# A Mamba and RWKV layer: scans that begin from zero, with the carry added into dbx by GpSimd

## The chip, the core and the metric

The kernel runs on one core of a Trainium2 chip. Such a core has five engines with instruction queues of their own: TensorE (PE, matrix products and transposes, which write to PSUM), VectorE (DVE), ScalarE (ACT), GpSimd (POOL) and SyncE (SP, which here issues the transfers). They run at the same time and wait for one another through semaphores. The metric is the device time of one launch in microseconds, from three runs; a separate run under the hardware profiler gives the trace that the rows below come from. Of that trace a row "in a view by line" gives a source line, an engine, what is written and read, how often, the busy time and the mean time of one; a row of a timeline gives the start, the duration and the same names.

## The reference, cut to what matters

The input is x of 4 x 2048 x 256 in fp32. The layer is a layer norm, a selective state-space block (Mamba) with a second layer norm behind it, a residual, a third layer norm and an RWKV channel mix. The part that costs most is the scan over the tokens, with 16 states for each of 256 channels:

```python
delta = softplus(delta_raw @ W_dt + b_dt)
A = -exp(A_log)
dA  = exp(einsum('bld,dn->bldn', delta, A))
dBx = einsum('bld,bln->bldn', delta * x, B_ssm)
def step(h, inp):
    dA_t, dBx_t, C_t = inp
    h = dA_t * h + dBx_t
    y_t = einsum('bdn,bn->bd', h, C_t)
    return (h, y_t)
```

Around it stand `y + x * D`, the gate `y * silu(z)`, the product with W_out, the norms, and the channel mix `sigmoid(xr @ W_r) * (relu(xk @ W_k)**2 @ W_v)`, where xr and xk mix each token with the one ahead of it.

## The kernel before

The 8192 tokens are cut into 16 chunks of 512, four to a sequence (`NT = 16`, `CPB = 4`). A step t of the main loop scans chunk t, prepares chunk t+1 (normalises it, turns it, makes delta, u = delta * x, B and C, z), finishes the Mamba block of chunk t-1 and the channel mix of chunk t-2. Steps 0 and 15, a short step ahead and a closing part are cut down versions of it.

Within a step there are 16 *columns*, one for each state n. A column is 128 partitions x 2 halves (of the 256 channels) x 512 tokens, and it takes:

- ScalarE: two exponentials, `da_ps<-delta,a_neg` (`exps`, line 662), each into one of three PSUM banks of a ring. The exponential of half-column k needs the bank that half-column k-3 used, so ScalarE may be at most three half-columns ahead. In a turn of 32 *places* (two for each column) ScalarE makes the exponential of column n+1 at place 2n + half, and then whatever else its table `ACT_TURN` puts at that place.
- GpSimd: `dbx<-u,b_ring` (`times_b`, line 543), one instruction of 128x1024, three columns ahead (`B_LEAD = 3`) into a ring of four (`X_RING = 4`).
- VectorE: two scans, `tensor_tensor_scan` (line 1045), one for each half, with state = da * state + dbx. Their start value is the constant 0.0 where a sequence begins (t divisible by 4) and otherwise `carry[:, n, h:h + 1]`, one number for each partition, that ScalarE copied out of the chunk ahead (`keep_carries`, line 668, and `keep_split_carry`, line 673).
- The product with C, `hg<-...,c_ring`: for *whole* columns GpSimd makes it (line 556, 128x1024, from SBUF into SBUF, one column behind); for *split* columns, listed in `SPLITS`, the scan stays in PSUM and VectorE makes the product, as one of 128x1024 (line 1052) where another piece of work stands between scan and product, as two of 128x512 (line 1061) otherwise. Even steps have 8 split columns, odd steps 9.
- TensorE: eight transposes of 128x128 that add the column to y (line 1331), up to two columns behind.

The other work of a step is placed by hand: `ACT_TURN` and `VEC_TURN` give a place from 0 to 31 to each stage of ScalarE and VectorE, `PE_TURN` a column to each of TensorE's, `BANK` one of three PSUM banks. Three stages of ScalarE change the function table, by `preload_act_table_set` in the code: `sp` at place 10 loads the softplus table, makes delta and loads the table with exp and tanh; `ln_exp` at place 20 loads the table with ln and exp. After that come the stages that take an inverse root by ln and exp (`rs1`, `rs2`, `rs3`; lines 620 and 622). The stage `tanh` (line 731) stands at place 19. Within one place the code runs through the stages in a fixed order, in which `rs1` stands ahead of `tanh`, and `tanh` ahead of `ln_exp`.

SyncE loads B and C in groups of four columns into rings of two groups (`load_b`, `load_c`), each after the last reader of the slot.

## Time and profile before

| | us |
|---|---|
| median of three runs | 941.3 (941.04 to 941.36) |
| the profiled execution | 941.56 |
| its span, first to last instruction | 939.8 |
| mean granted TensorE clock, share of full | 0.978 |

| engine | busy us | share |
|---|---|---|
| PE | 858.4 | 91% |
| DVE | 900.5 | 96% |
| ACT | 837.5 | 89% |
| POOL | 890.4 | 95% |

The span is nearly the whole of the time, so what is read from the trace carries over. A duration of two or more instructions in a timeline runs from the first start to the last end; the next instruction often starts some 0.07 us before the last one ends, so what an instruction costs its engine is the distance from start to start (called pitch below). `L1144`, VectorE's gate, runs once in a step at nearly the same place; it starts at 93.5 us in step 1 and at 866.8 us in step 15, so 14 turns take 773.3 us, 55.24 us each. This stretch is called the steady part.

### The profile page before, as it was taken

How to read it: one execution, taken by the hardware profiler on the slowest of the kernel's cores; microseconds unless marked ns; L12 is line 12 of the kernel's file. 1: busy time of each engine (PE TensorE's matmuls, PEld its weight loads, DVE VectorE, ACT ScalarE, POOL GpSimd, SP SyncE). 2: the span in 40 equal slices, each digit the busy share in tenths (PEclk: the TensorE clock that was granted, in tenths of full speed). 3: DMA queues.
4: the chain of work that ended last, by engine and by line, in shares of the span. 5: the costliest groups of instructions: out<-in, count | busy, mean ns of one | idle time of the engine just before them, and what ended most of it. 6: DMA issues, size and time to landing. Idle time of an engine off the chain costs nothing.

```text
span 939.8 us, 15796 instructions
## 1 busy us (share of the span) xinstructions
PE 858.4 (91%) x5024; PEld 685.0 (73%) x5024; DVE 900.5 (96%) x986; ACT 837.5 (89%) x2007; POOL 890.4 (95%) x413
## 2 busy tenths in 40 slices
PE   8766679989999898989999898998999899899998
PEld 5545466867878586776868678786878768678876
DVE  5899999999999999999999999999999999999896
ACT  4776889999999999998999999998999999978875
POOL 4999999999999999999999999999999999999980
PEclk9977899999999999999999999999999999999999
DMA  7345435462644644454374634446354454445231
GB/s 229 149 179 204 180 135 205 180 242 103 226 157 156 225 178 159 183 190 181 150 248 156 224 140 174 166 179 248 144 194 182 144 195 180 157 161 224 90 103 45
DMA packets 49939, 163.60 MB, mean 174 GB/s; under 512 B 5249, under 2 KB 33153, under 8 KB 33601
## 3 DMA queue, kind: packets, MB, share of 16 engines
q1 hardware_dynamic: 48528, 161.27, 46.0%
q0 software_dynamic: 512, 1.31, 0.5%
q8 instruction: 40, 0.66, 0.3%
q14 instruction: 43, 0.34, 0.1%
q10 hardware_dynamic: 816, 0.02, 0.1%
HBM read 153.15 MB, written 9.44 MB: 173 GB/s over the span
## 4 chain that ended last, share of the span: by engine, by line
PE 40%; ACT 27%; DVE 20%; issue 11%; POOL 1%; POOLq 0%; DVEq 0%; ACTq 0%
PE w_ps L1340 9%; ACT da_ps L662 9%; PE y_ps L1331 8%; DVE da_ps L1045 7%; PE w_ps L1364 5%; DVE hg L1045 4%; PE w_ps L1373 4%; PE w_ps L1376 4%; DVE hg L1052 4%; DVE hg L1061 3%; PE w_ps L1479 2%; ACT h_tok L599 2%; ACT zs L723 2%; PE w_ps L1382 2%; ACT xn_tok L599 2%
## 5 line engine op out<-in xcount | busy, mean ns | idle before, releaser
L543 POOL TENSOR_TENSOR dbx<-u,b_ring 128x1024 f32<-128x1024 f32 x255 | 599.7, 2379 | 2.0 <-DVE hg L1045 1.9
L662 ACT ACTIVATE da_ps<-delta,a_neg 128x512 f32<-128x512 f32 x512 | 340.2, 684 | 25.9 <-DVE hg L1052 8.6
L556 POOL TENSOR_TENSOR hg<-hg,c_ring 128x1024 f32<-128x1024 f32 x122 | 290.2, 2379 | 7.5 <-ACT carry L668 6.7
L1331 PE MATMUL y_ps<-ident,hg 128*128 128x128 f32 x2048 | 261.8, 278 | 10.4 <-POOL hg L556 10.2
L1331 PEld LDWEIGHTS y_ps<-ident,hg 128*128 128x128 f32 x2048 | 239.9, 144 | 37.4 <-issue 17.8
L1045 DVE TENSOR_TENSOR_SCAN da_ps<-da_ps,carry,dbx 128x512 f32<-128x512 f32 x203 | 249.5, 1270 | 3.5 <-ACT da_ps L662 3.5
L1045 DVE TENSOR_TENSOR_SCAN hg<-da_ps,carry,dbx 128x512 f32<-128x512 f32 x181 | 220.3, 1264 | 2.1 <-ACT carry L668 1.7
L1052 DVE TENSOR_TENSOR hg<-da_ps,c_ring 128x1024 f32<-128x1024 f32 x68 | 82.3, 1210 | 0.2
L1061 DVE TENSOR_TENSOR hg<-da_ps,c_ring 128x512 f32<-128x512 f32 x130 | 82.3, 673 | 0.0
L1045 DVE TENSOR_TENSOR_SCAN da_ps<-da_ps,dbx 128x512 f32<-128x512 f32 x64 | 75.4, 1211 | 3.4 <-ACT da_ps L662 3.1
L1045 DVE TENSOR_TENSOR_SCAN hg<-da_ps,dbx 128x512 f32<-128x512 f32 x64 | 74.8, 1206 | 2.4 <-ACT da_ps L662 2.4
L1340 PE MATMUL w_ps<-xnT_ring,w_in 128*128 128x512 f32 x120 | 61.7, 638 | 16.0 <-ACT xT L704 14.1
L1373 PE MATMUL w_ps<-w_rT,mixed 128*128 128x256 f32 x240 | 61.7, 380 | 0.0
L1376 PE MATMUL w_ps<-w_r_prev,mixed 128*128 128x256 f32 x240 | 61.6, 379 | 0.0
L1364 PE MATMUL w_ps<-w_in,xnT_ring 128*128 128x256 f32 x248 | 59.4, 382 | 0.9 <-ACT delta L696 0.6
L1340 PE MATMUL w_ps<-xnT_ring,w_dtx 128*128 128x512 f32 x120 | 57.9, 606 | 0.9 <-ACT bc_rows L808 0.9
L1364 PE MATMUL w_ps<-w_out,gated 128*128 128x256 f32 x248 | 58.7, 379 | 0.0
L1340 PE MATMUL w_ps<-mixed,w_kT 128*128 128x512 f32 x120 | 57.3, 601 | 0.0
L1364 PEld LDWEIGHTS w_ps<-w_in,xnT_ring 128*128 128x128 f32 x248 | 45.5, 190 | 15.0 <-ACT kact L690 4.9
L1373 PEld LDWEIGHTS w_ps<-w_rT,mixed 128*128 128x128 f32 x240 | 44.4, 190 | 11.4 <-issue 6.7
L1364 PE MATMUL w_ps<-w_vT,kact 128*128 128x256 f32 x232 | 52.6, 379 | 0.0
L1376 PEld LDWEIGHTS w_ps<-w_r_prev,mixed 128*128 128x128 f32 x240 | 45.6, 190 | 6.2
(214 smaller groups left out, 1320.7 us busy)
## 6 DMA issues: line engine op xcount, KB each, us to landing
c_ring<-bc_rows_dram SPq DMA_DIRECT2D x64, 1024.0 KB, 4.6
b_ring<-bc_rows_dram SPq DMA_DIRECT2D x63, 1024.0 KB, 6.6
xres<-in_L_attn_x_in_dram SPq DMA_DIRECT2D x16, 512.0 KB, 4.7
x_tok<-in_L_attn_x_in_dram SPq DMA_DIRECT2D x15, 512.0 KB, 6.0
out_dram<-r_out SPq DMA_DIRECT2D x14, 512.0 KB, 3.2
bc_rows_dram<-bc_rows SPq DMA_DIRECT2D x64, 16.0 KB, 5.4
w_in<-in_L_attn_W_in_dram SPq DMA_DIRECT2D x2, 256.0 KB, 4.3
x_tok<-in_L_attn_x_in_dram SPq DMA_DIRECT2D x2, 256.0 KB, 4.6
```

The source lines that it names most:

```text
L543: pool.tensor_tensor(dbx[:, n % X_RING, :, :], u[:, ip, :, :], b.to_broadcast([P, KH, LC]), ALU.mult).then_inc(s["dbx_done"], 1)
L556: pool.tensor_tensor(part, part, c_of(n).to_broadcast([P, KH, LC]), ALU.mult).then_inc(s["g_pool"], 1)
L599: last = act.activation(dst[j], src[j], ACT.Identity, scale=rs[j], bias=nm[j])
L662: act.activation(da_of(n, h), delta[:, ip, h, :], ACT.Exp, scale=a_neg[:, h, n:n + 1]).then_inc(s["da_ready"], 1)
L1045: dve.tensor_tensor_scan(out, da_of(n, h), dbx[:, n % X_RING, h, :], 0.0 if first else carry[:, n, h:h + 1], ALU.mult, ALU.add).then_inc(s ...
L1052: dve.tensor_tensor(hg[:, n % H_RING, :, :], da_both(n), c_of(n).to_broadcast([P, KH, LC]), ALU.mult).then_inc(s["g_vec"], 1)
L1061: last = dve.tensor_tensor(hg[:, n % H_RING, h:h + 1, :], da_ps[:, at:at + 1, :], c_of(n), ALU.mult)
L1331: last = pe.matmul(y_tok[:, b, h * P:(h + 1) * P], hg[:, n % H_RING, h, b * P:(b + 1) * P], ident[:, :], is_transpose=True, start=n == 0 a ...
L1340: last = pe.matmul(out, w[:, k, cols], x[:, k, :], start=k == 0, stop=k == KH - 1)
L1364: last = pe.matmul(by_block(out)[:, b, :], xT_[:, k, tokens], w[:, k, :], start=b == 0 and k == 0 and not begun, stop=k == KH - 1, skip_gr ...
L1373: pe.matmul(by_block(out)[:, b, :], h_of[:, k, at_b + 1:at_b + 1 + P], w_rT[:, k, :], start=k == 0, stop=False)
L1376: last = pe.matmul(by_block(out)[:, b, :], h_of[:, k, at_b:at_b + P], w_r_prev[:, k, :], start=False, stop=k == KH - 1)
```

## The change

Every scan now starts from 0.0. For chunks that continue a sequence, the start value is put in through the first token instead: da of the first token times the carry is added to dbx of the first token. For it

- ScalarE makes `first_a`, the exponential of delta's first token for all 16 states: two instructions of 128x16 right behind softplus in the stage `sp` (`first_decays`), in the 12 steps ahead of a chunk that continues a sequence;
- GpSimd multiplies carry and first_a for eight columns at a time (`weigh_carries`, 128x16, two for a chunk) and adds the product to the first tokens of two columns at a time (`hand_over`, 128x4, eight for a chunk), one of its places after it has made the two columns;
- GpSimd makes dbx for two columns in one instruction of 128x2048 (`times_b_twice`), except columns 0 and 1 of chunk 0. The ring grows to six columns, and the lead to four;
- VectorE's scan waits for `handed_over` where it waited for the carry;
- all even steps get column 3 as a ninth split column;
- places and banks are set anew, among them `rs1` from 22 to 19, `k0` from 9 to 8, `z1` from 11 to 13 on ScalarE, `gate` from 8 to 9, `u1` from 22 to 20 on VectorE, `xD`, `v0` and `v1` on TensorE; SyncE's loads stand in another order. Some semaphores of the closing part are shared between its two halves.

`C_RUN = 1` means that GpSimd's product with C is still one column an instruction. The core of the diff:

```diff
-X_RING = 4
+X_RING = 6
+HAND, WEIGH = 2, 8
+C_RUN = 1
-B_LEAD, C_LAG, Y_LAG = 3, 1, 2
+B_LEAD, C_LAG, Y_LAG = 4, 1, 2
-SPLITS = [[0, 2, 5, 6, 8, 11, 12, 14], [0, 2, 3, 5, 6, 8, 11, 12, 14]]
+SPLITS = [[0, 2, 3, 5, 6, 8, 11, 12, 14], [0, 2, 3, 5, 6, 8, 11, 12, 14]]
-                sum1=15, sq1=16, x0=18, tanh=19, ln_exp=20, rs1=22, x1=22, sq20=22, sq21=23, rs2=23, k1=24, square=24,
+                sum1=15, sq1=16, x0=18, tanh=19, ln_exp=20, rs1=19, x1=22, sq20=22, sq21=23, rs2=23, k1=24, square=24,
...
+            def weigh_carries(i, ip, n):
+                part = slice(n, n + WEIGH)
+                need(pool, s["first_a_set"], KH * firsts(i))
+                need(pool, s["carry_split"], kept_splits(i - 1, n + WEIGH - 1))
+                need(pool, s["carry_saved"], kept_wholes(i - 1, n + WEIGH - 1))
+                pool.tensor_tensor(handed[:, part, :], carry[:, part, :], first_a[:, ip, part, :],
+                                   ALU.mult).then_inc(s["handed_set"], 1)
+            def hand_over(i, ip, n):
+                pool.wait_ge(s["dbx_done"], NS * i + n + HAND)
+                pool.wait_ge(s["handed_set"], NS // WEIGH * (firsts(i) - 1) + n // WEIGH + 1)
+                at = dbx_of(i, n)
+                first = dbx[:, at:at + HAND, :, 0]
+                pool.tensor_tensor(first, first, handed[:, n:n + HAND, :], ALU.add).then_inc(s["handed_over"], 1)
+            def times_b_twice(i, ip, n):
...
+                need(pool, s["scan_done"], KH * (NS * i + n + 1 - X_RING + 1))
+                at, row = dbx_of(i, n), n % GN
+                b = b_ring[:, n // GN % BG, row:row + 2, :]
+                pool.tensor_tensor(dbx[:, at:at + 2, :, :], u[:, ip, :, :].unsqueeze(1).to_broadcast([P, 2, KH, LC]),
+                                   b.unsqueeze(2).to_broadcast([P, 2, KH, LC]), ALU.mult).then_inc(s["dbx_done"], 2)
...
+            def first_decays(i, ip):
+                need_all_read(act, i - 1, ["dt0", "dt1"])
+                for h in range(KH):
+                    act.activation(first_a[:, ip, :, h], a_neg[:, h, :], ACT.Exp,
+                                   scale=delta[:, ip, h, 0:1]).then_inc(s["first_a_set"], 1)
...
                         act.preload_act_table_set(EXP_TANH)
+                        if (t + 1) % CPB:
+                            first_decays(t + 1, nxt)
...
-                    dve.tensor_tensor_scan(out, da_of(n, h), dbx[:, n % X_RING, h, :],
-                                           0.0 if first else carry[:, n, h:h + 1], ALU.mult, ALU.add).then_inc(s["scan_done"], 1)
+                    dve.tensor_tensor_scan(out, da_of(n, h), dbx[:, dbx_of(t, n), h, :],
+                                           0.0, ALU.mult, ALU.add).then_inc(s["scan_done"], 1)
```

How the instructions stand in the two built programs, at three places. A row gives its number on the engine, the line, the operation, what is written and read, and its shape.

ScalarE, places 18 to 23 of a turn, ahead of the change (exponentials of columns 10 to 12; xT is the stage `x0` or `x1`, r_out is `tanh`, lv and rs are an inverse root, h_tok is `sq20`):

```order
302 L662 ACTIVATE da_ps<-delta,a_neg 128x512 x2
303 L704 ACTIVATE xT<-w_ps,d_par 128x512
304 L662 ACTIVATE da_ps<-delta,a_neg 128x512
305 L731 ACTIVATE r_out<-w_ps 128x512 x2
306 L662 ACTIVATE da_ps<-delta,a_neg 128x512
307 L873 ACT_TABLE_LOAD
308 L662 ACTIVATE da_ps<-delta,a_neg 128x512 x2
309 L668 ACTIVATE carry<-hg 128x4
310 L620 ACTIVATE lv<-sq,eps 128x4
311 L622 ACTIVATE rs<-lv 128x4
```

The same place behind the change:

```order
336 L726 ACTIVATE da_ps<-delta,a_neg 128x512 x2
337 L774 ACTIVATE xT<-w_ps,d_par 128x512
338 L726 ACTIVATE da_ps<-delta,a_neg 128x512
339 L684 ACT_TABLE_LOAD
340 L684 ACTIVATE lv<-sq,eps 128x4
341 L686 ACT_TABLE_LOAD
342 L686 ACTIVATE rs<-lv 128x4
343 L801 ACTIVATE r_out<-w_ps 128x512 x2
344 L726 ACTIVATE da_ps<-delta,a_neg 128x512
345 L945 ACT_TABLE_LOAD
```

The inverse root now stands ahead of tanh and of the load of line 945, and the built program has a table load ahead of its logarithm and another ahead of its exponential, which no line of the code asks for. Both stand there in steps 0 to 13, 14 times; the loads of the old places are all still there.

GpSimd in the middle of a chunk that continues a sequence, ahead of the change and behind it:

```order
50 L543 TENSOR_TENSOR dbx<-u,b_ring 128x1024 [waits u1_done,scan_done,u0_done,b_loaded3] x2
51 L556 TENSOR_TENSOR hg<-hg,c_ring 128x1024 [waits carry_saved,c_loaded2]
52 L543 TENSOR_TENSOR dbx<-u,b_ring 128x1024 [waits u1_done,scan_done,u0_done,b_loaded3]
53 L556 TENSOR_TENSOR hg<-hg,c_ring 128x1024 [waits carry_saved,c_loaded2]
54 L543 TENSOR_TENSOR dbx<-u,b_ring 128x1024 [waits u1_done,scan_done,u0_done,b_loaded3]
```

```order
49 L590 TENSOR_TENSOR dbx<-dbx,handed 128x4
50 L600 TENSOR_TENSOR dbx<-u,b_ring 128x2048
51 L615 TENSOR_TENSOR hg<-hg,c_ring 128x1024
52 L590 TENSOR_TENSOR dbx<-dbx,handed 128x4
53 L600 TENSOR_TENSOR dbx<-u,b_ring 128x2048
54 L615 TENSOR_TENSOR hg<-hg,c_ring 128x1024
55 L590 TENSOR_TENSOR dbx<-dbx,handed 128x4
```

Two columns of dbx became one instruction, and a small addition stands between them and the next two.

VectorE at columns 9 to 11, behind the change (the order of these is as before, but that the second `u` stood one column later, and the scans read carry):

```order
239 L1114 SCALAR_TENSOR_TENSOR hg<-da_ps,dbx 128x512 [waits y_added,da_ready,handed_over,dbx_done]
240 L1114 SCALAR_TENSOR_TENSOR hg<-da_ps,dbx 128x512 [waits da_ready]
241 L1114 SCALAR_TENSOR_TENSOR hg<-da_ps,dbx 128x512 [waits y_added,da_ready,handed_over,dbx_done]
242 L1114 SCALAR_TENSOR_TENSOR hg<-da_ps,dbx 128x512 [waits da_ready]
243 L1151 TENSOR_TENSOR u<-w_ps,delta 128x512 [waits work_ready0,work_read0]
244 L1114 SCALAR_TENSOR_TENSOR da_ps<-da_ps,dbx 128x512 [waits y_added,da_ready,handed_over,dbx_done]
245 L1114 SCALAR_TENSOR_TENSOR da_ps<-da_ps,dbx 128x512 [waits da_ready]
```

The scans are named SCALAR_TENSOR_TENSOR here. Whole columns 9 and 10, the stage `u1`, then split column 11 follow one another with no product of VectorE between them. Over the whole program the change makes 127 instructions of 128x2048 for dbx out of 254 of its 255 of 128x1024, leaves 114 products on GpSimd (122 before), adds 24 of 128x16 and 96 of 128x4 there, and leaves 16 products of 128x1024 and 250 of 128x512 on VectorE (68 and 130 before).

## Rows read from the trace of the kernel before

**Rows 1.** The page's engine totals; busy time by engine in the steady part
```profile
PE 858.4 (91%) x5024; PEld 685.0 (73%) x5024; DVE 900.5 (96%) x986; ACT 837.5 (89%) x2007; POOL 890.4 (95%) x413
...
core 0: us, PE busy (x) PEld busy (x) DVE busy (x) ACT busy (x) POOL busy (x), PEclk, DMA share, GB/s
93.50:866.80 773.30, 722.34 (x4290) 581.40 (x4289) 763.36 (x798) 721.97 (x1758) 764.60 (x343) 0.99 0.49 181
```

**Rows 2.** Timeline of ScalarE at places 19 to 22 of step 8
```profile
555.46 0.68 ACT L662 ACTIVATE da_ps<-delta,a_neg 128x512 f32<-128x512 f32 x1
556.07 1.07 ACT L731 ACTIVATE r_out<-w_ps 128x512 f32<-128x512 f32 x2
557.03 0.70 ACT L662 ACTIVATE da_ps<-delta,a_neg 128x512 f32<-128x512 f32 x1
557.74 1.28 ACT L873 ACT_TABLE_LOAD   x1
559.04 1.30 ACT L662 ACTIVATE da_ps<-delta,a_neg 128x512 f32<-128x512 f32 x2
...
560.37 0.28 ACT L620 ACTIVATE lv<-sq,eps 128x4 f32<-128x4 f32 x1
560.69 0.20 ACT L622 ACTIVATE rs<-lv 128x4 f32<-128x4 f32 x1
```

**Rows 3.** Timeline of VectorE in the same stretch, columns 8 to 11
```profile
552.21 1.21 DVE L1052 TENSOR_TENSOR hg<-da_ps,c_ring 128x1024 f32<-128x1024 f32 x1
553.33 0.68 DVE L1082 TENSOR_TENSOR u<-w_ps,delta 128x512 f32<-128x512 f32 x1
553.93 4.79 DVE L1045 TENSOR_TENSOR_SCAN hg<-da_ps,carry,dbx 128x512 f32<-128x512 f32 x4
558.65 2.44 DVE L1045 TENSOR_TENSOR_SCAN da_ps<-da_ps,carry,dbx 128x512 f32<-128x512 f32 x2
```

**Rows 4.** Groups of VectorE by line and form: scans into PSUM, from a carry and from zero
```profile
L1045 DVE TENSOR_TENSOR_SCAN da_ps<-da_ps,carry,dbx 128x512 f32<-128x512 f32 x203 | 249.5, 1270 | 3.5 <-ACT da_ps L662 3.5
...
L1045 DVE TENSOR_TENSOR_SCAN da_ps<-da_ps,dbx 128x512 f32<-128x512 f32 x64 | 75.4, 1211 | 3.4 <-ACT da_ps L662 3.1 <-POOL dbx L541 0.3
```

**Rows 5.** Timeline of VectorE where step 7 passes into step 8
```profile
514.03 2.32 DVE L1045 TENSOR_TENSOR_SCAN da_ps<-da_ps,dbx 128x512 f32<-128x512 f32 x2
516.26 1.26 DVE L1061 TENSOR_TENSOR hg<-da_ps,c_ring 128x512 f32<-128x512 f32 x2
517.44 1.21 DVE L1045 TENSOR_TENSOR_SCAN hg<-da_ps,dbx 128x512 f32<-128x512 f32 x1
...
521.26 2.46 DVE L1045 TENSOR_TENSOR_SCAN da_ps<-da_ps,carry,dbx 128x512 f32<-128x512 f32 x2
523.63 1.26 DVE L1061 TENSOR_TENSOR hg<-da_ps,c_ring 128x512 f32<-128x512 f32 x2
```

**Rows 6.** Groups of GpSimd by line and form
```profile
L543 POOL TENSOR_TENSOR dbx<-u,b_ring 128x1024 f32<-128x1024 f32 x255 | 599.7, 2379 | 2.0 <-DVE hg L1045 1.9
...
L561 POOL TENSOR_TENSOR nr<-nm,rs 128x4 f32<-128x4 f32 x14 | 3.0, 217 | 0.0
...
L541 POOL TENSOR_TENSOR dbx<-u,b_ring 128x512 f32<-128x512 f32 x1 | 1.3, 1262 | 0.9 <-DVE u L1082 0.9
...
L505 POOL TENSOR_SCALAR_AFFINE_SELECT ident<-ident 128x128 f32<-128x128 f32 x1 | 0.3, 283 | 0.2 <-POOL ident L503 0.2
```

**Rows 7.** Timeline of GpSimd around its one small instruction of a step
```profile
511.66 2.37 POOL L543 TENSOR_TENSOR dbx<-u,b_ring 128x1024 f32<-128x1024 f32 x1
513.97 0.22 POOL L561 TENSOR_TENSOR nr<-nm,rs 128x4 f32<-128x4 f32 x1
514.13 4.69 POOL L543 TENSOR_TENSOR dbx<-u,b_ring 128x1024 f32<-128x1024 f32 x2
```

**Rows 8.** Timelines of ScalarE and VectorE at the softplus stage of step 8
```profile
541.76 1.28 ACT L816 ACT_TABLE_LOAD   x1
...
543.26 0.69 ACT L662 ACTIVATE da_ps<-delta,a_neg 128x512 f32<-128x512 f32 x1
...
542.74 2.54 DVE L1045 TENSOR_TENSOR_SCAN da_ps<-da_ps,carry,dbx 128x512 f32<-128x512 f32 x2
```

**Rows 9.** Group of ScalarE by line: one of three table loads of a step
```profile
L813 ACT ACT_TABLE_LOAD x15 | 19.2, 1283 | 0.3
```

140 lines of the change are left out of this document (84 added, 56 removed).

## The prediction

> **What bounds the kernel now.** I read the engine totals first, then the same totals for the steady part alone (14 turns of 55.24 us) [rows 1]. There VectorE is busy 763.4 us and GpSimd 764.6 of 773.3, both near 99%; ScalarE is busy 722.0 and so idle for 51.3, or 3.7 us a turn. Two engines are full, and the third has little to spare. Next come the timelines of ScalarE and VectorE side by side [rows 2, 3], because the exponentials have only three PSUM banks: ScalarE can never be more than three half-columns, some 3.5 us of scans, ahead of VectorE. A pause of ScalarE longer than that is a pause of VectorE, whatever the share of busy time says. Let half-column (n, h) be half h of column n. The exponential at 555.46 is that of (10, 1), which needs the bank of (9, 0). That scan ran from 553.93 to about 555.1 (four scans in 4.72 us, 1.18 each) [rows 3], so ScalarE was then within 0.35 us of its farthest lead. It made tanh and (11, 0), done at 557.73 [rows 2]; VectorE read it at 558.65. The spare time there is 0.9 us.
>
> **VectorE: scans from zero.** Scans from a carry take 1270 ns and from zero 1211 in the groups by form [rows 4]. By start-to-start times a pair from zero costs 2.23 us (514.03 to 516.26) and a pair from a carry 2.37 (521.26 to 523.63) [rows 5]: 0.07 us a scan, 0.067 with other pairs of these turns. 384 scans lose it: -25.7. Column 3 of eight even steps comes over: two halves at 1.18 us (516.26 to 517.44) [rows 5], +9.4. And 52 products that were one instruction of 1.12 us (552.21 to 553.33) [rows 3] become two halves at 1.18, since their place holds no other work now: 52 x 0.05 = +2.6. VectorE's work changes by -13.7 us. The 32 scans of the last step don't count, because GpSimd, which gets more to do there, has no idle time in it to speak of: +2.1. This leaves -11.6.
>
> **GpSimd.** A column of dbx takes 2379 ns, the one half column of its kind 1262 [rows 6]: 1117 for 512 elements, and a fixed part of 2379 - 2 x 1117 = 145 ns. One of two columns saves that once: 127 x 0.145 = -18.4. Eight products at 2.31 us (511.66 to 513.97) [rows 7] go: -18.5. For the small ones the nearest row is the 128x4 instruction, which costs 0.16 us from start to start (513.97 to 514.13) [rows 7]: 96 x 0.16 = +15.4. The 24 of 128x16 are taken as 0.19: +4.6. Three hand-overs of a chunk stand (nearly) behind the very instruction whose result they wait for; an instruction that waited for its own engine's last result sat idle for 0.2 us [rows 6], and with the overlap of 0.07 us lost, that is 36 x 0.25 = +9. Sum: about -8 us, if none is dearer; the bounds are 0.16 and, with 0.2 of idle time on either side of each, 0.6 us. No wait of VectorE comes from it: two columns are made once the scan five columns ahead of the second is done, take 4.5 us, and with one product and the hand-over they are ready some 7 us later, while VectorE has four columns, over 13 us, to do. In the head and in step 0 it is the same instructions in another grain, at nothing.
>
> A rule on the price of the pair: the Trainium skill, GPSIMD Engine Reference, section "Performance versus the Vector engine", gives 4497 ns for a two-input operation of 2048 fp32. With the rows' durations the pair is 4613 ns; by the page's figure it would save another 0.12 us, 15 us of GpSimd's time in all. That would matter only if GpSimd were the bound, and it isn't in what follows.
>
> **ScalarE: two table loads that the places bring.** `rs1` moved from place 22 to 19, ahead of tanh and of the load at place 20. The table there is the one with exp and tanh, without ln, and the built program loads a table ahead of the logarithm and again ahead of the exponential. Every table load of the trace takes 1283 ns [rows 9], 1.30 from start to start (557.74 to 559.04) [rows 2]. Logarithm and exponential cost 0.32 (560.37 to 560.69) and about 0.15 [rows 2]. So between exponential (10, 1) and (11, 0) come 2 x 1.29 + 0.32 + 0.15 = 3.05 us that weren't there. In the timeline (11, 0) would be done at 557.73 + 3.05 = 560.8. VectorE is ready for it earlier than before in one respect and later in another: four scans from zero end by 553.93 + 4.48 = 558.4, and `u1`, now in between, costs 0.60 (553.33 to 553.93) [rows 3], so 559.0. **It waits 1.8 us.** The next exponential, (11, 1), comes 2.0 us behind (11, 0), because the load of `ln_exp` lies between them (557.73 to 559.74) [rows 2]; the scan of (11, 0) covers 1.12 of these: 0.85 more. Together 2.6; if ScalarE gets to (10, 1) 0.35 us earlier, as the bank allows, 2.25. It can't get there earlier still: the ring is the limit. I take 2.4, in 13 of the 14 steps with the loads (+31.2); in step 0 VectorE waits anyway for others.
>
> **ScalarE: softplus.** The exponential (6, 1) starts at 543.26 and ends when VectorE needs it: the two scans at 542.74 span 2.54 us where 2.46 is usual [rows 5, 8]. No time is spare. The change adds two small exponentials (0.2 each) and a wait for softplus's own result (0.2) in that stage, and takes `k0` (0.6) out of the place ahead of it. Between nothing and 0.8 us of new wait; the middle, 0.4, for 12 steps: +4.8. One more carry copy in even steps (8 x 0.2) lies in idle time.
>
> **TensorE and SyncE.** Their work stays; y is added up to 2 us later for odd columns behind a pair, against a ring of eight columns. B's loads are asked for one column sooner, behind a slot that is also free one column sooner. I set both at nothing; if the cover were gone it would show as waits on `y_ps` or on a load.
>
> **The sum.** 941.56 - 11.6 + 31.2 + 4.8 = 966.0. VectorE's old idle time in the steady part, 9.9 us [rows 1], is partly waits which a longer wait next to them takes up: half, -5. That is 961.0 for a profiled execution, and 0.3 less, **960.7**, for a median. Check by ScalarE's load: 722.0 + 13 x 2.58 + 11 x 0.6 + 1.4 = 764 in the steady part, which would then be about 793 long. So it isn't full, but it stands still while the ring is closed.
>
> **A rule that speaks for more.** The two bare loads of a turn are followed by work 1.30 us after their start [rows 2]. The Trainium skill, ScalarE: Activation LUTs, section "What ACT_TABLE_LOAD costs", puts a drain of 1380 ns on top of the 1283 ns. With it the two loads would cost 2.76 us more, 13 x 2.76 = 36 us, and the time would be 997. The trace shows no such time behind its loads, so I give it 0.02. By the same page, section "Table sets: the hidden batching unit", ln and then exp need one load, since one set has both; the built program has two, and the program is what runs.
>
> **Rivals.**
> - *The new loads are hidden* (0.10, faster). If a table load cost nothing at this place because it ran while the engine waited for its bank (or if the two didn't run), then only -11.6 and about +1 of frictions remain: 931. For it speaks that ScalarE has 3.7 us idle a turn; against it, that the lead is capped by three banks. It decides when the exponentials (10, 1) and (11, 0) are less than 3.9 us apart.
> - *ScalarE is full, but not in the way* (0.10, not slower). If the pause were made up by idle time that ScalarE has elsewhere, its 764 us of work and the idle 9.9 us that the fullest engine has today would make a steady part of 773 to 775: 941 to 943 us. It needs a lead longer than three half-columns, or place 19 to lie beside VectorE's long stages, which here are a column away.
> - *Hand-overs are dear* (0.06, slower). At 0.6 us each, a chunk that continues a sequence costs GpSimd 8 x 4.49 + 7 x 2.31 + 0.16 + 8 x 0.6 + 0.4 = 57.5 us, and with one from zero in four 56.2 a turn. That is as long as VectorE's turn with its new waits; the two together would give 966 to 975. Alone it turns from gain to loss at 0.4 us each.
> - *The forecast* (0.72), 948 to 972: its lower end has 1.6 us of wait at column 11 and none at softplus, its upper end 2.75 and 0.8.
>
> **The numbers.** Slower takes the forecast, the dear hand-overs, the drain and 0.04 of the second rival: 0.84. The same takes 0.06 of the second rival, faster the 0.10 of the first. I take 0.2% as what a measurement of this kernel can tell from no change. A range from 942 to 972 leaves out the first rival, a little of the second and what lies above.
>
> **What would show it.** Behind the change: a group of table loads at lines 684 and 686, 14 each at 1283 ns; VectorE idle ahead of the scans of column 11, released by ScalarE's exponential of line 726, some 30 us over the program; scans at 1.21 us or less, all of them; GpSimd's pair near 4.6 us by duration and busy time below 890 with idle time now; hand-overs near 0.22 us by duration; the turn from gate to gate near 56.6 us. I am wrong if the waits of VectorE for line 726 sum to under 15 us, if GpSimd has no idle time (then the hand-overs are dear), or if the turn is below 55.2.

## The result, and the profile after

The changed kernel takes **982.2 us** (median of three runs, 979.7 to 982.9), against 941.3: 1.043 times as long (95% interval 1.040 to 1.046), 40.9 us more. The profiled execution took 982.9 us with a span of 981.1. The forecast was 960.7 with a range up to 972, so the direction was right, but the time lies 10 us above the range, and the cost (40.9 us) is twice the forecast's (19.4).

The page's engine totals of the changed kernel, and busy time by engine in its steady part, now 97.8 to 908.8 (columns as in [rows 1]):

```profile
PE 871.7 (89%) x5024; PEld 682.0 (70%) x5024; DVE 893.4 (91%) x1054; ACT 876.4 (89%) x2067; POOL 874.2 (89%) x398
...
97.80:908.80 811.00, 736.95 (x4296) 579.37 (x4295) 756.46 (x859) 757.73 (x1814) 752.52 (x334) 0.99 0.48 172
```

Against [rows 1] VectorE has 7.1 us less to do, GpSimd 16.2 less, ScalarE 38.9 more, and the span is 41.3 longer. In the steady part 37.7 us of this were added (811.0 for 773.3; 57.9 a turn for 55.2). No engine is full any more: VectorE idles 54.5 us there, GpSimd 58.5, ScalarE 53.3. Three engines at 93% and none at 99% wait for one another in turns. The question is for whom, and the waits answer it (whole program; us in total, times, longest):

```profile
DVE da_ps L1114 <- ACT da_ps L726: 44.2, 41, 1.9
POOL dbx L600 <- DVE hg L1114: 32.6, 17, 3.5
POOL hg L615 <- ACT carry L732: 26.0, 10, 2.8
...
ACT kact L760 <- PE w_ps L1409: 15.9, 13, 1.4
...
DVE hg L1114 <- ACT da_ps L726: 6.0, 12, 1.5
```

VectorE waits for exponentials. GpSimd's waits are behind that: it waits for VectorE's scans and for the copies that ScalarE makes of them. The fourth line is one that I had not foreseen.

Timeline of ScalarE at places 18 to 21 of step 9 of the changed kernel, which answers to [rows 2]. (Counted by the scans, the rows that are headed step 8 above, [rows 2, 3, 8], are of step 9 too, and in [rows 5] step 8, whose scans start from zero, passes into step 9. No reading depends on it.)

```profile
581.83 0.68 ACT L726 ACTIVATE da_ps<-delta,a_neg 128x512 f32<-128x512 f32 x1
582.52 1.28 ACT L684 ACT_TABLE_LOAD   x1
583.82 0.30 ACT L684 ACTIVATE lv<-sq,eps 128x4 f32<-128x4 f32 x1
584.13 1.28 ACT L686 ACT_TABLE_LOAD   x1
585.43 0.20 ACT L686 ACTIVATE rs<-lv 128x4 f32<-128x4 f32 x1
585.54 1.06 ACT L801 ACTIVATE r_out<-w_ps 128x512 f32<-128x512 f32 x2
586.49 0.69 ACT L726 ACTIVATE da_ps<-delta,a_neg 128x512 f32<-128x512 f32 x1
587.21 1.28 ACT L945 ACT_TABLE_LOAD   x1
588.50 1.30 ACT L726 ACTIVATE da_ps<-delta,a_neg 128x512 f32<-128x512 f32 x2
```

And VectorE in the same stretch, which answers to [rows 3]; what stands in brackets is the idle time ahead of an instruction and what ended it:

```profile
580.30 4.55 DVE L1114 TENSOR_TENSOR_SCAN hg<-da_ps,dbx 128x512 f32<-128x512 f32 x4
584.77 0.66 DVE L1151 TENSOR_TENSOR u<-w_ps,delta 128x512 f32<-128x512 f32 x1
587.32 1.23 DVE L1114 TENSOR_TENSOR_SCAN da_ps<-da_ps,dbx 128x512 f32<-128x512 f32 x1 [1.88 <-ACT da_ps L726]
589.23 1.23 DVE L1114 TENSOR_TENSOR_SCAN da_ps<-da_ps,dbx 128x512 f32<-128x512 f32 x1 [0.68 <-ACT da_ps L726]
```

Exponential (10, 1) starts at 581.83 and (11, 0) at 586.49: 4.66 us apart, where it was 1.57 in [rows 2]. Of the 3.09 more, 3.02 are the two loads with logarithm and exponential (582.52 to 585.54). VectorE loses 1.88 and then 0.68 us. Each load is again 1.28 us, and 1.30 from its start to the next instruction's (582.52 to 583.82).

The softplus stage of the same step, ScalarE:

```profile
563.40 0.60 ACT L760 ACTIVATE kact<-w_ps 128x512 f32<-128x512 f32 x1 [1.20 <-PE w_ps L1409]
563.89 1.29 ACT L726 ACTIVATE da_ps<-delta,a_neg 128x512 f32<-128x512 f32 x2
...
565.33 1.28 ACT L883 ACT_TABLE_LOAD   x1
...
569.20 0.51 ACT L742 ACTIVATE first_a<-a_neg,delta 128x16 f32<-128x16 f32 x2
...
569.79 0.69 ACT L726 ACTIVATE da_ps<-delta,a_neg 128x512 f32<-128x512 f32 x1
```

and VectorE, which answers to [rows 8]:

```profile
568.02 1.22 DVE L1114 TENSOR_TENSOR_SCAN da_ps<-da_ps,dbx 128x512 f32<-128x512 f32 x1
570.52 1.23 DVE L1114 TENSOR_TENSOR_SCAN da_ps<-da_ps,dbx 128x512 f32<-128x512 f32 x1 [1.27 <-ACT da_ps L726]
```

Here ScalarE first stood still for 1.20 us, waiting for TensorE's product for `kact` (the stage `k0`, now at place 8 instead of 9), and only then went on to the softplus stage. VectorE waits 1.27 us for (6, 1).

Groups by line and form, the new instructions (answering to [rows 6, 9]; the scans stand further below):

```profile
L600 POOL TENSOR_TENSOR dbx<-u,b_ring 128x2048 f32<-128x2048 f32 x127 | 576.8, 4543 | 32.8 <-DVE hg L1114 32.6
...
L590 POOL TENSOR_TENSOR dbx<-dbx,handed 128x4 f32<-128x4 f32 x96 | 19.7, 205 | 2.0
...
L684 ACT ACT_TABLE_LOAD x14 | 18.0, 1283 | 0.2
L686 ACT ACT_TABLE_LOAD x14 | 18.0, 1283 | 0.2
...
L742 ACT ACTIVATE first_a<-a_neg,delta 128x16 f32<-128x16 f32 x24 | 6.1, 302 | 0.1
L581 POOL TENSOR_TENSOR handed<-carry,first_a 128x16 f32<-128x16 f32 x24 | 5.4, 226 | 0.0
```

### The profile page after: what moved, and what is told of

It reads as the page before. It is cut to its first block, busy times and chain, and to the rows that moved or that the text cites. A ratio compares the mean times of both kernels' runs of the same rounds, so it can differ in the third digit from the quotient of the medians.

```text
span 981.1 us, 15781 instructions
## 1 busy us (share of the span) xinstructions
PE 871.7 (89%) x5024; PEld 682.0 (70%) x5024; DVE 893.4 (91%) x1054; ACT 876.4 (89%) x2067; POOL 874.2 (89%) x398
## 4 chain that ended last, share of the span: by engine, by line
ACT 52%; PE 17%; issue 15%; DVE 14%; POOL 1%; DVEq 0%; ACTq 0%; POOLq 0%
ACT da_ps L726 17%; DVE hg L1130 4%; PE w_ps L1409 4%; DVE da_ps L1114 4%; PE y_ps L1400 3%; DVE hg L1114 3%; PE w_ps L1433 2%; ACT spare L677 2%; ACT xres L952 2%; ACT h_tok L677 2%; ACT L883 2%; ACT spare L669 2%; ACT L886 2%; ACT h_tok L663 2%; ACT L684 2%
## 5 line engine op out<-in xcount | busy, mean ns | idle before, releaser
L600 POOL TENSOR_TENSOR dbx<-u,b_ring 128x2048 f32<-128x2048 f32 x127 | 576.8, 4543 | 32.8 <-DVE hg L1114 32.6
L1114 DVE TENSOR_TENSOR_SCAN da_ps<-da_ps,dbx 128x512 f32<-128x512 f32 x283 | 334.1, 1215 | 50.2 <-ACT da_ps L726 44.2
L615 POOL TENSOR_TENSOR hg<-hg,c_ring 128x1024 f32<-128x1024 f32 x114 | 269.3, 2364 | 30.5 <-ACT carry L732 26.0
L1114 DVE TENSOR_TENSOR_SCAN hg<-da_ps,dbx 128x512 f32<-128x512 f32 x229 | 265.3, 1205 | 6.2 <-ACT da_ps L726 6.0
L1400 PE MATMUL y_ps<-ident,hg 128*128 128x128 f32 x2048 | 256.8, 276 | 15.8 <-POOL hg L615 15.8
L1400 PEld LDWEIGHTS y_ps<-ident,hg 128*128 128x128 f32 x2048 | 236.4, 143 | 42.6 <-POOL hg L615 17.7
L1130 DVE TENSOR_TENSOR hg<-da_ps,c_ring 128x512 f32<-128x512 f32 x250 | 158.5, 676 | 0.4 <-DMA c_ring<-bc_rows_dram 0.4
L1409 PE MATMUL w_ps<-mixed,w_kT 128*128 128x512 f32 x120 | 58.7, 613 | 4.6 <-DVE mixed L1167 4.0
L1433 PE MATMUL w_ps<-w_in,xnT_ring 128*128 128x256 f32 x248 | 58.7, 380 | 0.8 <-ACT delta L766 0.8
L1433 PE MATMUL w_ps<-w_out,gated 128*128 128x256 f32 x248 | 58.7, 379 | 0.0
L1442 PEld LDWEIGHTS w_ps<-w_rT,mixed 128*128 128x128 f32 x240 | 44.4, 190 | 11.6 <-issue 6.7
L1433 PEld LDWEIGHTS w_ps<-w_vT,kact 128*128 128x128 f32 x232 | 41.8, 190 | 12.0 <-ACT xres L952 7.5
L1433 PEld LDWEIGHTS w_ps<-w_out,gated 128*128 128x128 f32 x248 | 44.7, 190 | 4.8
L1409 PEld LDWEIGHTS w_ps<-xnT_ring,w_in 128*128 128x128 f32 x120 | 22.4, 198 | 34.3 <-issue 15.5
```

The lines of the kernel that those rows point to most:

```text
L600: pool.tensor_tensor(dbx[:, at:at + 2, :, :], u[:, ip, :, :].unsqueeze(1).to_broadcast([P, 2, KH, LC]), b.unsqueeze(2).to_broadcast([P, 2, ...
L615: pool.tensor_tensor(part, part, c_of(n, k).unsqueeze(2).to_broadcast([P, k, KH, LC]), ALU.mult).then_inc(s["g_pool"], k)
L1114: dve.tensor_tensor_scan(out, da_of(n, h), dbx[:, dbx_of(t, n), h, :], 0.0, ALU.mult, ALU.add).then_inc(s["scan_done"], 1)
L1130: last = dve.tensor_tensor(hg[:, n % H_RING, h:h + 1, :], da_ps[:, at:at + 1, :], c_of(n), ALU.mult)
L1400: last = pe.matmul(y_tok[:, b, h * P:(h + 1) * P], hg[:, n % H_RING, h, b * P:(b + 1) * P], ident[:, :], is_transpose=True, start=n == 0 a ...
L1409: last = pe.matmul(out, w[:, k, cols], x[:, k, :], start=k == 0, stop=k == KH - 1)
```

## The experiments

The theory: the time comes from two places of ScalarE's table, `rs1` at 19 with its two loads and `k0` at 8 with its wait; the rest of the change is about neutral or a small gain. The rival: it is the change of the scans (hand-overs, small exponentials, pairs), or the new order of the rest. Each ratio below is against the kernel before, run next to it; its median was 941.6 in the runs of the first group, 941.7 in those of the second and 942.3 in those of the third.

### One place back at a time, and the one place alone

**The inverse root back behind the third load**, in the changed kernel:

```diff
-... ln_exp=20, rs1=19, ...
+... ln_exp=20, rs1=22, ...
```

> The changed kernel with one number put back: rs1 at place 22 instead of 19, behind the load of the table with ln and exp. Theory 1 (the two table loads of lines 684 and 686 hold the exponentials of column 11 back, and a ring of three banks can't bridge it): the loads and the waits of 1.88 and 0.68 us a turn ahead of the scans of column 11 go, 14 turns x 2.5 = 35 us, so 947 us (944 to 952); the wait of 1.27 us ahead of (6,1) stays. Rival (GpSimd's hand-overs and pairs are what made it slower, as its 87 us of idle time that VectorE and ScalarE release could hide): no more than the 36 us of ScalarE's work go, none of it from the time: over 972 us.

Measured 947.0 us (945.6 to 948.7), 1.006 [1.004, 1.007]. Against the changed kernel, one number gives back 35.2 of the 40.9 us.

**k0 back by one place**, in the changed kernel:

```diff
-ACT_TURN = dict(... bc=6, k0=8, sp=10, ...
+ACT_TURN = dict(... bc=6, k0=9, sp=10, ...
```

> The changed kernel with one number put back: k0 at place 9 instead of 8. Theory 1 for the softplus stage: at place 8 ScalarE waits 1.2 us for TensorE's k0 (15.9 us over the program), and comes to the softplus stage that much later; at place 9 most of that wait goes, VectorE's 1.27 us ahead of (6,1) fall to 0.5 or less, and the time falls by 8 to 12 us to 970 to 975. Rival (the wait comes from the two added exponentials and the wait for softplus's result alone): the wait stays over 1 us and the time within 3 us of 982.

Measured 972.4 us (971.9 to 973.9), 1.033 [1.031, 1.034], 9.8 us under the changed kernel. Its waits, whole program:

```profile
DVE da_ps L1114 <- ACT da_ps L726: 36.4, 39, 1.9
...
ACT kact L760 <- PE w_ps L1409: 2.9, 13, 0.2
```

ScalarE's wait for TensorE fell from 15.9 to 2.9 us, and VectorE's for ScalarE by 7.8. At (6, 1), VectorE still waits 0.67 us in each of ten turns.

**The one number in the kernel before**, with nothing else of the change:

```diff
-... ln_exp=20, rs1=22, ...
+... ln_exp=20, rs1=19, ...
```

> The kernel before with one number changed: rs1 at place 19 instead of 22, everything else as it was. Theory 1: VectorE had 0.9 us to spare ahead of (11,0), so 3.05 us more on ScalarE leave a wait of 2.1 us there, and 0.8 ahead of (11,1): 14 turns x 2.9 = 41, less what old waits take up, 972 to 982 us. Rival (ScalarE's idle 3.7 us a turn take the loads up): 941 to 948 us.

Measured 979.8 us (978.8 to 980.6), 1.040 [1.039, 1.042]: 38.1 us from this alone. Its steady part and its wait:

```profile
94.90:904.00 809.10, 732.33 (x4294) 581.97 (x4294) 765.42 (x798) 755.79 (x1784) 766.11 (x343) 0.99 0.47 173
```

VectorE and GpSimd have the work that they had [rows 1], and ScalarE 33.8 us more, 13 times 2.6; the part is 35.8 us longer. In a turn VectorE now waits 2.23 + 0.62 us ahead of the scans of column 11. The inverse root moved to place 19 costs nearly the same with and without the rest of the change.

### What is left without the places

**All tables of before** (`ACT_TURN`, `VEC_TURN`, `PE_TURN`, `BANK`) in the changed kernel; scans from zero, hand-overs, pairs and the ninth split column stay:

```diff
-ACT_TURN = dict(prev=0, norm1=3, hT1=3, xnT1=5, xnT0=4, hT0=5, bc=6, k0=8, sp=10, z0=11, z1=13, gT0=11, gT1=12,
-                sum1=15, sq1=16, x0=18, tanh=19, ln_exp=20, rs1=19, x1=22, sq20=22, sq21=23, rs2=23, k1=24, square=24,
+ACT_TURN = dict(prev=0, norm1=3, hT1=3, xnT1=4, xnT0=4, hT0=5, bc=6, k0=9, sp=10, z0=11, z1=11, gT0=11, gT1=12,
+                sum1=15, sq1=16, x0=18, tanh=19, ln_exp=20, rs1=22, x1=22, sq20=22, sq21=23, rs2=23, k1=24, square=24,
...
-VEC_TURN = dict(mix1=5, mix0=7, gate=9, z0=13, z1=15, u0=17, u1=20, x20=24, x21=25, v0=30, v1=30)
+VEC_TURN = dict(mix1=5, mix0=6, gate=8, z0=12, z1=16, u0=17, u1=22, x20=24, x21=25, v0=31, v1=31)
...
```

> The changed kernel with the four tables of places and banks of the kernel before (ACT_TURN, VEC_TURN, PE_TURN, BANK); hand-overs, pairs, splits and loads as changed. Theory 1: no extra table loads, k0 at 9, so only what the change does by itself is left: 12 us less on VectorE, up to 0.6 us of wait at the softplus stage in 12 turns: 936 us (930 to 943). Rival (hand-overs are dear, or GpSimd's larger grain costs waits): 945 us or more.

Measured 947.4 us (945.8 to 948.9), 1.007 [1.005, 1.008]. This expectation failed: I had looked for a gain of 5, and the structural part of the change, put into the old places, costs 6. Its steady part:

```profile
93.20:871.40 778.20, 726.64 (x4293) 584.04 (x4292) 755.41 (x805) 724.31 (x1787) 752.36 (x334) 0.98 0.50 180
```

The work of both full engines did fall (VectorE from 763.4 to 755.4, GpSimd from 764.6 to 752.4), and the part got 4.9 us longer all the same, since VectorE's idle time there rose by 12.9. Its waits for exponentials rose by nearly as much over the whole program, from 6.6 to 15.8 us ahead of scans into PSUM and from 2.4 to 5.2 ahead of those into SBUF. The next three runs look for the reason.

**Scans from the constant alone**, in the kernel before:

```diff
-                                           0.0 if first else carry[:, n, h:h + 1], ALU.mult, ALU.add)
+                                           0.0, ALU.mult, ALU.add)
```

> The kernel before with the start value of every scan set to 0.0 and nothing else: the waits for the carries stay, the carry itself is left out (so chunks that continue a sequence begin anew). It takes 20 us off VectorE's work and touches no other engine. Theory 2 (ScalarE's exponentials, at most three half-columns ahead, and GpSimd at 99% hold VectorE at nearly the old pace in most places): most of it comes back as waits for da_ps and dbx, and the time is 934 to 938 us. Rival (VectorE is the bound of the old kernel): 920 to 925 us.

Measured 936.9 us (934.7 to 937.9), 0.994 [0.992, 0.996]. VectorE's work in the steady part fell by 15.9 us (763.4 to 747.5), the time by 4.9:

```profile
92.20:861.70 769.50, 724.33 (x4292) 584.78 (x4292) 747.49 (x798) 719.35 (x1759) 764.55 (x342) 0.98 0.49 182
```

GpSimd is busy 764.6 of 769.5 us, and this work alone allows no steady part shorter than that. But of VectorE's 22.0 us of idle time there (9.9 before) the profile puts none down to GpSimd: 12.1 are waits for exponentials (5.1 before), and 3.7 waits for ScalarE's copies of the carry (1.7 before), which this run keeps though nothing reads them. So the run shows that two engines close at hand, ScalarE by its lead and GpSimd by its work, take the gain back, and not which of them would do so alone. Of what was taken off VectorE, less than a third became time.

**The other half alone**: the kernel with the old tables, but scans begin from the carry and nothing is handed over:

```diff
-                        if (t + 1) % CPB:
-                            first_decays(t + 1, nxt)
...
-                    if made_before and made_before[0] % CPB and made_before[2] % HAND == 0:
-                        hand_over(*made_before)
...
-                                           0.0, ALU.mult, ALU.add).then_inc(s["scan_done"], 1)
+                                           0.0 if first else carry[:, n, h:h + 1], ALU.mult, ALU.add).then_inc(s["scan_done"], 1)
```

> The changed kernel with the old tables of places and banks, scans from the carry as before (the wait for the carry too), and without first_a, the products of carry and first_a, and the hand-overs: what is left of the change is dbx by twos, the ring of six, the lead of four, the order of loads and the ninth split column. VectorE then has 7 products of 1.12 us more in the steady part than before (763 + 8 = 771 us of work) and GpSimd 33 less. Theory (the pairs cost nothing by themselves): VectorE's added work and no more, 947 to 951 us. Rival (the larger grain makes waits of its own): VectorE waits for dbx or y, over 953 us.

Measured 948.6 us (947.4 to 949.2), 1.007 [1.005, 1.009]. Here GpSimd is relieved (735.8 of 779.5) and VectorE full, with the ninth split column in the even steps:

```profile
93.50:873.00 779.50, 729.12 (x4296) 583.82 (x4295) 771.57 (x804) 722.40 (x1765) 735.81 (x224) 0.98 0.49 179
```

So pairs and a ninth column make room on GpSimd at VectorE's cost, and scans from zero make room on VectorE. Scans from zero gain less than the work of their engine says, and pairs with a ninth column lose nearly what VectorE's added work says (6.2 us of the steady part for 8.2 of work), so that the 28.8 us taken off GpSimd gain 2 us at most.

**The small exponentials four places later**, in the kernel with the old tables:

```diff
-                        if (t + 1) % CPB:
-                            first_decays(t + 1, nxt)
...
+                    if pre and not start and place == 14 and (t + 1) % CPB:
+                        first_decays(t + 1, nxt)
```

> The changed kernel with the old tables of places and banks (947.4 us) and first_a made at place 14 instead of within the softplus stage at place 10. Theory 1: the wait of 0.66 us ahead of the exponential (6,1) falls to 0.2 or less in 12 turns, 940 to 943 us. Rival (VectorE is early there because its scans are shorter, and would wait wherever the 0.6 us lie): the waits move to column 8 or 9 and the time stays at 946 to 948 us.

Measured 944.3 us (941.9 to 945.6), 1.002 [1.001, 1.003], between what the two theories gave. The wait at (6, 1) fell from 0.66 to 0.27 us a turn, but the one at (11, 1) rose from 0.30 to 0.66, and in all VectorE's waits for `da_ps` rose by 0.9 (15.8 to 16.7) where those of the scans into SBUF fell by 3.6. Part of the wait moved, part of it went.

### All three places mended

The changed kernel with `rs1` at 22, `k0` at 9 and the small exponentials at 14 (called the mended kernel below):

```diff
-... k0=8, ... rs1=19, ...
+... k0=9, ... rs1=22, ...
...
-                        if (t + 1) % CPB:
-                            first_decays(t + 1, nxt)
+                    if pre and not start and place == 14 and (t + 1) % CPB:
+                        first_decays(t + 1, nxt)
```

> The changed kernel with three places: rs1 back at 22, k0 back at 9, first_a at place 14 instead of in the softplus stage. Theory 1: of 947.0 us with rs1 at 22, the wait of 1.27 us ahead of (6,1) falls to 0.1 in 12 turns: 933 to 937 us, which would beat the kernel before. Rival (waits move on instead of going): 941 us or more.

Measured 934.8 us (934.8 to 939.4), 0.993 [0.991, 0.996]: 47.4 us under the changed kernel, 6.9 under the one before. Its steady part:

```profile
94.60:860.70 766.10, 719.25 (x4294) 578.86 (x4293) 753.95 (x860) 724.73 (x1787) 751.75 (x334) 0.99 0.50 182
```

VectorE's work is that of the changed kernel less 2.5; 12.2 us of idle time are left. Its waits for exponentials are 5.9 us ahead of scans into PSUM and 5.3 ahead of those into SBUF in the whole program (8.2 together in the steady part), and ScalarE's wait at `k0` is 2.9 us in all. This kernel differs from that of the run ahead of it (old tables, small exponentials at 14, 944.3 us) only in the other places and banks of the change: those are a gain of 9 us, or of 5 by the runs that follow.

The same kernel once more, with no edit, in five more runs:

> The best version so far once more, unchanged, on the same chip as the others of this call, since one of its four runs lay at 939.4: 934 to 936 us, and faster than the kernel before by 0.6 to 0.8% in every round.

Measured 939.2 us (937.4 to 939.4), 0.996 [0.995, 0.997]. Faster than before once more, but the expectation failed: 3.1 us for 6.9. Both groups of runs leave it faster than the kernel before by more than 0.2%; between 0.993 and 0.996 the runs don't decide.

The same kernel with eight split columns in even steps again:

```diff
-SPLITS = [[0, 2, 3, 5, 6, 8, 11, 12, 14], [0, 2, 3, 5, 6, 8, 11, 12, 14]]
+SPLITS = [[0, 2, 5, 6, 8, 11, 12, 14], [0, 2, 3, 5, 6, 8, 11, 12, 14]]
```

> The best version so far with eight split columns in even steps again (column 3 to GpSimd): 8 products of 1.18 us off VectorE, 8 of 2.31 on GpSimd, whose 752 us in the steady part become 768 where the whole part is 766 now. Theory: GpSimd is then full and sets the pace, 937 to 943 us. Rival (VectorE and ScalarE still set it): 928 to 934 us.

Measured 942.0 us (940.0 to 944.6), 1.000 [0.999, 1.001]. Its steady part:

```profile
98.10:865.70 767.60, 717.84 (x4279) 578.67 (x4278) 746.98 (x845) 723.47 (x1781) 764.81 (x340) 0.99 0.51 181
```

GpSimd is full again, and the ninth split column is worth 2.9 us (942.0 less 939.2). The traces show where, and it isn't in the steady turns: the steady part is 767.6 us long with eight columns and 768.4 with nine. The two profiled executions differ by 6.9 us in their spans (942.7 and 935.8). The gate of step 1 comes 3.0 us later (98.1 for 95.1), of which 2.1 stand already ahead of the first scan, and what follows the gate of step 15 takes 77.0 us for 72.3. There TensorE waits 4.1 us for GpSimd's product with C (0.9 with nine columns), `tanh` comes late by it, and VectorE waits 5.7 us for one exponential, (5, 1), instead of 0.9. So a full GpSimd costs time where the last step leaves it no turn to catch up in; that it sets the pace of a turn, as the theory had it, isn't shown.

### Does a load cost its time anywhere?

The theory said that two loads cost because they fall where VectorE is about to need the next exponential, and that elsewhere some of ScalarE's idle time would take them up. To separate the loads from the inverse root, two bare loads (which nothing needs, and behind which the table is the one of before) went into the mended kernel, in the steps 0 to 13, once at place 19 and once at place 25:

```diff
+                    if more and not start and place == 19:
+                        act.preload_act_table_set(LN_EXP)
+                        act.preload_act_table_set(EXP_TANH)
```

> The best version so far (the changed kernel with rs1 at 22, k0 at 9, first_a at place 14: 934.8 us) with two bare table loads added at place 19, ahead of tanh, in steps 0 to 13; the inverse root stays at 22. Theory 1 (the loads alone, at a place where three half-columns of lead are all there is): 2.58 us on ScalarE against 1.2 us that VectorE has to spare, and the 0.68 of the exponential behind the next load: 2.1 us a turn, 962 to 966 us. Rival (it is the inverse root at place 19, not the loads): under 940 us.

Measured 966.8 us (965.0 to 969.0), 1.026 [1.024, 1.028]: 27.7 us above the mended kernel of the same group.

```diff
+                    if more and not start and place == 25:
+                        act.preload_act_table_set(EXP_TANH)
+                        act.preload_act_table_set(LN_EXP)
```

> The same two loads at place 25, after the exponential (13,1), where VectorE has an affine stage of 0.8 us, a product of 1.13 and another affine stage between its scans. Theory 1 (it is the place): the pause fits into VectorE's other work for the most part, 936 to 944 us. Rival (ScalarE has no idle time worth the name, so 2.58 us cost the same wherever they stand): 2.2 us a turn and more, 962 us or above.

Measured 990.2 us (987.5 to 992.0), 1.051 [1.049, 1.052]: 51.1 us above it. This expectation failed, and on the other side: the place of the timeline that looked the roomier was the dearer. The steady parts, at place 19:

```profile
96.60:895.00 798.40, 728.64 (x4295) 578.40 (x4294) 756.67 (x860) 759.09 (x1814) 753.88 (x335) 0.99 0.48 175
```

at place 25:

```profile
97.50:917.90 820.40, 742.48 (x4295) 595.54 (x4294) 759.69 (x860) 761.79 (x1813) 750.41 (x331) 0.96 0.46 169
```

and with neither, in the five runs above:

```profile
95.10:863.50 768.40, 719.56 (x4293) 578.82 (x4292) 754.40 (x860) 725.39 (x1787) 751.33 (x334) 0.99 0.49 181
```

For 13 x 2.6 = 33.5 us of loads there are 30.0 us more at place 19 and 52.0 at place 25: 2.3 and 4.0 us a turn for 2.6 us of loads. At place 25 the pause also reaches TensorE. The waits of that kernel, of which the first is 19.1 us with the loads at 19, the second 4.0, the third 35.6, the fourth 5.3, the fifth 2.4, and the last isn't there:

```profile
POOL dbx L600 <- DVE hg L1117: 51.6, 32, 3.2
...
PE w_ps L1436 <- ACT xres L955: 36.6, 13, 3.1
...
DVE da_ps L1117 <- ACT da_ps L726: 25.9, 28, 2.1
DVE hg L1117 <- ACT da_ps L726: 21.1, 27, 1.5
...
DVE w_ps L1179 <- PE w_ps L1436: 16.4, 12, 2.5
ACT r_out L972 <- PE w_ps L1565: 15.7, 22, 2.3
```

TensorE waits 36.6 us for ScalarE's instruction on `xres`, some 3 us in each of twelve turns, where it is 0.4 with the loads at 19. VectorE then waits for TensorE's product, and ScalarE for another. TensorE's granted clock was also lower there, 0.96 of full (2.4 GHz) in the steady part against 0.99, with PE's busy time 22.9 us longer than in the kernel without loads.

The turns of this one trace let the clock be told from the place. With the loads at 25, the granted clock falls to its lower level (1.2 GHz) in every turn from step 3 to step 13, each time about where TensorE's wait of 3 us for `xres` ends. In steps 3, 6, 9 and 12 it stays there for 6.8 us, and in the other seven for 3.4. With the loads at 19, and with none, it stays at 2.4 GHz in all these turns. The turns of steps 9 and 10 at place 25, from gate to gate (columns as in [rows 1]):

```profile
569.49:629.57 60.08, 55.05 (x313) 44.08 (x312) 54.77 (x63) 55.97 (x137) 54.18 (x27) 0.94 0.45 168
629.57:688.46 58.89, 53.86 (x313) 42.99 (x312) 54.78 (x64) 55.55 (x133) 54.23 (x27) 0.97 0.45 172
```

The four turns with 6.8 us at the lower level take 59.9 to 60.1 us, the seven with 3.4 us take 58.5 to 58.9: 1.3 us for 3.4 us of slow clock. VectorE's waits for ScalarE are the same in both kinds (3.2 us in most), those for TensorE some 2.0 in the one and 0.7 to 1.1 in the other. If the first 3.4 us cost what the second do (an estimate from these turns), the clock makes 15 x 1.3 = 20 of the 52 us, and what is left, 32, is close to the 30.0 of place 19. The one turn at place 25 with the full clock around its loads, that of step 2, says the same: 58.2 us, against 58.4 with the loads at 19 and 55.6 with none. TensorE waits 3.1 us in that turn too. So the pause itself seems to cost about as much at either place, and what made place 25 dearer is, for the most part, the slower clock behind TensorE's wait. No run holds the clock fixed; the division is read from the turns of one execution.

## Why the prediction was right in its direction and too low

**The two loads (right).** The term was 2.4 us in 13 turns, +31.2. The waits of VectorE ahead of column 11 sum to 31.2 us in the changed kernel, 1.88 + 0.68 in the step shown. That the sum fits so exactly is in part luck: it is 2.5 us a turn in twelve turns, and 0.6 in each of the first two. In three turns the profile names GpSimd's dbx instead (5.7 us, the wait of 1.89 us each time at this very place): there the pair, late by GpSimd's own wait for VectorE, lands 0.13 us behind the late exponential, and with `rs1` at 22 neither is late. The undoing (35.2 us) and the number alone (38.1) confirm that this is the cause, and the two bare loads at place 19 (27.7 us) that most of it is the loads and not the inverse root. A count of half-columns, not a busy share, gave its size. The drain that would have made it 36 us more isn't there: the next instruction starts 1.30 us after the load does, as the rows above show. (The Trainium skill, ScalarE: Activation LUTs, section "What ACT_TABLE_LOAD costs", puts 1380 ns on top; the traces of this case disagree.)

**Softplus (wrong, the largest miss).** The term was +4.8 for 0.4 us of wait at (6, 1), between 0 and 0.8; in the steady part it measured 15.2 us in all (1.1 before): 1.27 in most turns, and 0.55 even in steps 3, 7 and 11, which make no `first_a`. The step that failed is "takes `k0` (0.6) out of the place ahead of it": a stage moved forward was booked as time saved, without a look at whether its input is there so early. It isn't, and it came even later than before. TensorE's product for `k0` keeps its column, but what it waits for moved: its own input is `mixed`, which VectorE's stage `mix0` makes, and the change put `mix0` at place 7 instead of 6. And ScalarE's `xnT1`, which TensorE needs for the products ahead of that one, went from place 4 to 5. VectorE and TensorE in step 9, ahead of the change:

```profile
533.93 0.73 DVE L1098 SCALAR_TENSOR_TENSOR mixed<-w_ps,muk,mixed 128x512 f32<-128x512 f32 x1
534.71 1.99 PE L1340 MATMUL w_ps<-mixed,w_kT 128*128 128x512 f32 x4
```

and behind it:

```profile
560.58 0.74 DVE L1167 SCALAR_TENSOR_TENSOR mixed<-w_ps,muk,mixed 128x512 f32<-128x512 f32 x1
561.38 1.98 PE L1409 MATMUL w_ps<-mixed,w_kT 128*128 128x512 f32 x4 [0.21 <-DVE mixed L1167]
```

Counted from the first scan of column 3 (531.57 and 557.15) the product starts 3.14 us in ahead of the change and 4.23 behind it, 1.1 us later. Of this some 0.7 are there already in the product ahead of it, for which TensorE waited 0.66 us for `xnT_ring`; the rest is `mixed`. ScalarE reached `k0` at 562.20 and waited 1.20 us, so with `mix0` and `xnT1` at their old places nearly all of that wait would have gone (an estimate; no run puts these two back alone). Over the program ScalarE stood 15.9 us in 13 turns at `k0` (1.0 in the kernel before). With `k0` back at 9 the time fell by 9.8 us. The cost of the small exponentials was also put too low: with `k0` at 9 they stand behind most of the 0.67 us that VectorE still waits, since with them at place 14 this wait is 0.27, and the forecast had 0.4 with `k0` counted as a gain.

**VectorE's work (right in kind, too large).** Scans: forecast -25.7, measured -20.6. The groups of the scans in the changed kernel are:

```profile
L1114 DVE TENSOR_TENSOR_SCAN da_ps<-da_ps,dbx 128x512 f32<-128x512 f32 x283 | 334.1, 1215 | 50.2 <-ACT da_ps L726 44.2 <-POOL dbx L600 5.7 <-POOL dbx L570 0.3
...
L1114 DVE TENSOR_TENSOR_SCAN hg<-da_ps,dbx 128x512 f32<-128x512 f32 x229 | 265.3, 1205 | 6.2 <-ACT da_ps L726 6.0
```

A scan from zero is 0.056 us shorter than one from a carry by the mean of all (1211 ns against 1267), not 0.067 as read from a few pairs: 21.5 us. And a scan that begins behind idle time doesn't overlap the end of the one ahead; in the mended kernel, with few such waits, the same groups are down by 22.5. Products: forecast +12.0, measured +13.3. VectorE's work is down by 7.1 us in all, where the sum had 11.6 (13.7, less 2.1 for the last step): 4.5 us of the miss.

**The waits that were to be absorbed (wrong).** The forecast let the new waits take up 5 us of VectorE's old idle time. What is left over when all other terms are taken off the measured 41.3 us is -1.0: 4.0 us of the miss. This term is had by difference and not read from a row, and the halving had no row behind it either.

**Column 1 (not forecast).** ScalarE is now late at (1, 0) too, by 0.34 us in nine turns, 3.0 us in all. Why is open.

These account for the profiled execution: 961.0 + 10.4 (softplus) + 3.0 (column 1) + 4.5 (work) + 4.0 (the remainder) + 0.0 (column 11) = 982.9, which comes out by construction, since the remainder is taken as what closes it.

**GpSimd (right).** A pair takes 4543 ns, forecast 4.6; by what the Trainium skill gives in GPSIMD Engine Reference, section "Performance versus the Vector engine", it would be 4497, a little under the measured one. The hand-over took 205 ns by duration and 0.14 from start to start, as this timeline shows, in which the second line is GpSimd's next pair:

```profile
547.78 0.19 POOL L590 TENSOR_TENSOR dbx<-dbx,handed 128x4 f32<-128x4 f32 x1
547.92 4.54 POOL L600 TENSOR_TENSOR dbx<-u,b_ring 128x2048 f32<-128x2048 f32 x1
```

GpSimd's work fell by 16.2 us where I had 8, and the rival of dear hand-overs falls. The sum had 9 us for hand-overs that wait for the result right ahead of them, and all 96 together show 2.0 us of idle time ahead of them. GpSimd has idle time now and isn't the bound.

**The rivals.** That the loads are hidden falls with the first timeline. The rival "ScalarE is full, but not in the way" falls too, and the reason that I had given for it was the better one: ScalarE's 757.7 us of work left room in a part of 773, and the time was lost because it can't be done ahead. The two bare loads show that its idle share isn't room at either place that was tried: at neither did a load come for free.

**What the forecast's sum would have said of the structural part alone** is -11.6. Mended, it is -6.9 or -3.1; in the old places it is +5.8. What the forecast left out is that ScalarE gets no faster: when VectorE and GpSimd need less time for a turn, exponentials that came just in time are late. In the mended kernel such waits are 8.2 of the 12.2 us that VectorE idles in the steady part. (The mended kernel isn't the structural part alone: it keeps the other new places.)

## What to carry to other kernels

When a stage moves across a switch of the function table, count the loads in the built program, not in the source, and hold their time against how far ahead the ring lets ScalarE be: here one changed number brought two loads a step and 35 to 38 us. When a stage moves forward, ask first whether its producer, and the producer's own input, have moved, and which way; a move that looks like time taken out of a busy place can be a wait put in. Take work off an engine only after counting how many are full: with two full, 15.9 us off one gave 4.9 us of time, and both halves together needed their places set right before they gained anything. And look at the granted clock, turn by turn, before a longer time is put down to a place: part of it can be TensorE at the lower clock behind a wait.
